# Second feed-forward of a two-layer macaron block: the bias moved from GpSimd into TensorE products, and ScalarE's normalisation of the next group moved ahead

## What is computed

```
x = x + 0.5 * _L0_ffn_ref(_layernorm(x, axis=-1), L0_ffn_kernel, L0_ffn_bias, L0_ffn_a, L0_ffn_b)
...
    w = simulate_quantize_int4(kernel)
    y = jnp.einsum('bsd,df->bsf', x, w) + bias
    lora = jnp.einsum('bsr,rf->bsf', jnp.einsum('bsd,dr->bsr', x, a), b)
    return y + lora
```

```
ri = jnp.concatenate([xf, _stats(xf)], -1)
h = jax.nn.gelu(ri @ r1_w.T + r1_b, approximate=False)
probs = jax.nn.softmax(h @ r2_w.T, -1)
```

## Time and profile before

| | before |
|---|---|
| median of three runs | 1788.64 us |
| profiled execution: its own time | 1788.87 us |
| profiled execution: its span | 1787.2 us |
| TensorE matmul busy in the span | 1488.8 us (83%) |
| VectorE, ScalarE, GpSimd busy | 977.1, 728.9, 564.3 us |
| granted clock of TensorE, mean of the span | 0.908 of full |

### The profile page before, as it was taken

The page is one execution under the profiler, slowest core; times in us unless marked ns, Lnnn a source line. Parts: engine busy times, 40 slices in busy tenths (PEclk is TensorE's granted clock), DMA queues, the critical chain, the costliest instruction groups (busy, mean ns, idle before and its releaser), DMA issues. The chain is left out here.

```text
span 1787.2 us, 27066 instructions
## 1 busy us (share of the span) xinstructions
PE 1488.8 (83%) x9512; PEld 1127.3 (63%) x9512; DVE 977.1 (55%) x2816; ACT 728.9 (41%) x1775; POOL 564.3 (32%) x467
## 2 busy tenths in 40 slices
PE   6899989999999678339999997489995459999994
PEld 5566544555554454229889997255553349899994
DVE  8865677787873597855531111356566855521110
ACT  5222147666667375415423232114333425322331
POOL 6522210000000442321636455221211231636535
PEclk9989889999999898559999999699997569999997
DMA  3034363333300022325969894401112326879974
GB/s 104 18 127 129 107 131 63 79 55 79 55 26 1 12 95 83 150 44 174 246 194 258 245 246 65 133 25 35 48 36 95 118 71 201 225 221 247 265 193 47
DMA packets 113493, 212.11 MB, mean 119 GB/s; under 512 B 20085, under 2 KB 79386, under 8 KB 104154
## 3 DMA queue, kind: packets, MB, share of 16 engines
q1 hardware_dynamic: 87066, 178.93, 31.8%
q0 software_dynamic: 26304, 31.60, 11.4%
HBM read 158.71 MB, written 51.38 MB: 118 GB/s over the span
## 5 line engine op out<-in xcount | busy, mean ns | idle before, releaser
L952 DVE TENSOR_REDUCE attnm_top<-psum 128x1 f32<-128x384 f32 (+3 forms) x384 | 212.8, 597 | 56.4 <-PE psum L1037 52.3
L1174 ACT ACTIVATE attnm_prob<-psum 128x512 f32<-128x512 f32 (+1 forms) x384 | 192.1, 530 | 87.6 <-PE psum L1047 81.0
L2328 POOL DMA_INDIRECT x_sum<-moe1e_y,moe_scatter_i x76 | 119.7, 1575 | 128.2 <-ACT moe1e_y L2462 71.0
L2507 DVE SCALAR_TENSOR_TENSOR moe1e_h<-moe1e_gate,psum 128x160 f32<-128x160 f32 x160 | 50.6, 321 | 199.4 <-ACT moe1e_gate L2436 199.1
L2328 POOL DMA_INDIRECT out<-moe2e_y,moe_scatter_i x76 | 119.2, 1568 | 127.7 <-ACT moe2e_y L2462 70.5
L2507 DVE SCALAR_TENSOR_TENSOR moe2e_h<-moe2e_gate,psum 128x160 f32<-128x160 f32 x160 | 50.4, 321 | 198.8 <-ACT moe2e_gate L2436 198.6
L2383 PE MATMUL psum<-moe1e_xgT,moe_w_up 128*128 128x160 f32 x1024 | 152.2, 304 | 2.4 <-ACT moe1e_xgT L2452 2.4
L2383 PE MATMUL psum<-moe2e_xgT,moe_w_up 128*128 128x160 f32 x1024 | 150.7, 302 | 2.4 <-ACT moe2e_xgT L2452 2.4
L2383 PEld LDWEIGHTS psum<-moe1e_xgT,moe_w_up 128*128 128x128 f32 x1024 | 144.2, 193 | 4.8 <-issue 4.8
L2383 PEld LDWEIGHTS psum<-moe2e_xgT,moe_w_up 128*128 128x128 f32 x1024 | 142.7, 192 | 4.8 <-issue 4.8
L1348 POOL DMA_INDIRECT moe_xg<-xn_rows,moe_gather_i x80 | 84.3, 1054 | 159.3 <-DVE moe_gather_i L1536 93.0
(11 more groups left out here) (414 smaller groups left out, 3230.5 us busy)
## 6 DMA issues: line engine op xcount, KB each, us to landing
moe_w_up<-in_expert_up SPq DMA_DIRECT2D x64, 1024.0 KB, 7.5
moe_w_down<-in_expert_down SPq DMA_DIRECT2D x64, 512.0 KB, 3.5
attnm_q_hat<-q_parts SPq DMA_DIRECT2D x72, 128.0 KB, 4.4
moe_a_up<-in_adapter_up SPq DMA_DIRECT2D x32, 256.0 KB, 4.2
q_parts<-attnf_q_part SPq DMA_DIRECT2D x12, 512.0 KB, 2.8
attnm_k_hat<-k_parts SPq DMA_DIRECT2D x72, 64.0 KB, 2.3
x_res<-in_x SPq DMA_DIRECT2D x8, 512.0 KB, 9.4
v_tails<-attnf_v_tail SPq DMA_DIRECT2D x4, 1024.0 KB, 4.3
```

Of the source, the lines that this page charges most:

```text
L952: nc.vector.tensor_reduce(top[:, n // QUADS % 2, tiles[0]:tiles[-1] + 1, hh:hh + 1], s.ps[:, u.bank, 0:len(tiles) * width].rearrange("p (t ...
L1174: nc.scalar.activation(prob[:, i % NPROB, at:GROUP], s.ps[:, u.bank, at:GROUP], ACT.Exp).then_inc(taken[u.bank], 1)
L2328: nc.gpsimd.indirect_dma_start(total, bass.IndirectOffsetOnAxis(ap=rows, axis=0), y[:, q, k, :], None, bounds_check=TOKENS + SPARE - 1, oo ...
L2507: nc.vector.scalar_tensor_tensor(out=h[:, n % 2, i, :], in0=gate[:, i, :], scalar=1.0 if i < INTER // P else SCALE_A, in1=s.ps[:, u.bank, ...
```

## The change

The bias is no longer added by GpSimd. GpSimd clears a tile `ffn_bias_row` of 128 partitions and copies the bias into its partition 0, once. TensorE opens each of the two banks of multiply(g) with a product of 128x512: the stationary side is column 0 of the identity, repeated 128 times (ones in row 0, zeros in the other 127), the moving side is `bias_row`, repeated twice; the eight products with `ffn_w` then add to it. TensorE waits for the row before the first step of its list. update(g) no longer waits for GpSimd. Apart from that, norm(i+3) on ScalarE moves from behind copy_x(i-1) to directly behind copy(i+2).

```diff
+    bias_row = st.sb("bias_row", [P, C])
...
         @block.gpsimd
         def _(pool):
-            def bias(g):
-                pool.wait_ge(normed, g + 1)
-                xg = s.x[:, GT * g:GT * g + GT, :]
-                nc.gpsimd.tensor_tensor(xg, xg, s.ffn_bias[:].rearrange("p (o c) -> p o c", o=1)
-                                        .broadcast_to([P, GT, C]), ALU.add).then_inc(biased, 1)
-
             for n, part in enumerate(PARTLY):
...
-            bias(0)
-            bias(1)
+            nc.gpsimd.memset(bias_row[:], 0.0).then_inc(cleared, 1)
+            pool.wait_ge(cleared, 1)
+            nc.gpsimd.tensor_copy(bias_row[0:1, :], s.ffn_bias[0:1, :]).then_inc(row_made, 1)
             for i in range(GROUPS):
-                if i + 2 < GROUPS:
-                    bias(i + 2)
                 r.rstd(pool, i)
...
-                v.wait_ge(biased, g + 1)
...
-                for k in range(GT):
-                    for c in range(CC):
-                        mm = nc.tensor.matmul(s.ps[:, u.bank + k // 2, (k % 2) * C:(k % 2 + 1) * C],
-                                              xnT[:, g % 2, c, k * P:(k + 1) * P], s.ffn_w[:, c, :],
-                                              start=(c == 0), stop=(c == CC - 1))
+                for a in range(2):
+                    nc.tensor.matmul(s.ps[:, u.bank + a, :].rearrange("p (h c) -> p h c", c=C), s.ident[:, 0:1].broadcast_to([P, P]),
+                                     bias_row[:].rearrange("p (o c) -> p o c", o=1).broadcast_to([P, 2, C]),
+                                     start=True, stop=False, skip_group_check=True)
+                    for k in range(2 * a, 2 * a + 2):
+                        for c in range(CC):
+                            mm = nc.tensor.matmul(s.ps[:, u.bank + a, (k % 2) * C:(k % 2 + 1) * C],
+                                                  xnT[:, g % 2, c, k * P:(k + 1) * P], s.ffn_w[:, c, :],
+                                                  start=False, stop=(c == CC - 1), skip_group_check=True)
...
+            pe.wait_ge(row_made, 1)
             for what, g in ORDER:
...
                 if 0 <= i + 2 < GROUPS:
                     copy(i + 2)
+                if 0 <= i + 3 < GROUPS:
+                    norm(i + 3)
                 if 0 <= i - 1 < GROUPS:
                     r.absolute(act, i - 1)
...
                     r.copy_x(act, i - 1)
-                if 0 <= i + 3 < GROUPS:
-                    norm(i + 3)
```

More of the change, by code:

```diff
@@ L1892, in ffn_router @@
     shift = st.sb("shift", [P, TILES])
+    bias_row = st.sb("bias_row", [P, C])
     r = RouterFront(nc, st, s, m)
     sem = st.sem
-    all_var, all_rstd, shifted, normed, biased, dve = (sem(n) for n in ("all_var", "all_rstd", "shifted", "normed", "biased", "dve"))
+    all_var, all_rstd, shifted, normed, cleared, row_made, dve = (
+        sem(n) for n in ("all_var", "all_rstd", "shifted", "normed", "cleared", "row_made", "dve"))
     banks = Banks(st)
```

## The result

The changed kernel takes 1796.14 us (median of nine runs, 1793.78 to 1803.79) against 1787.43 of the kernel before (nine runs); the ratio is 1.0043, 95% interval 1.003 to 1.0055. In a second series the changed kernel had 1.0061 (1.0041 to 1.0081). It is slower, by 8 us in the first series and 11 in the second; forecast were 10 (1799, 0.6%), counted from the 1788.64 us of the first three runs of the kernel before. The profiled execution took 1799.05 us.

A forecast was written before the change was run, and what follows sets the result against it. Rounds were taken to close over TensorE and ScalarE, not VectorE. update(7) was 4.26 + 3.26 + 0.73 + 1.73 = +9.98 us; 1788.87 + 10.0 gave about 1799, own range 1796 to 1801, 8-in-10 range 1794.5 to 1803.

The forecast's parts named there:

- The row: Start of the stage: TensorE waits for the bias row ahead of turn(0), +2.6 us (2.4 to 2.8).
- The products: In multiply: 0.865 us a product, 1.73 us a group; update(0) at +4.6 us, update(1) at +6.3.
- the dear product: Rival in multiply: a repeated column or row makes a product cost 1.7 us instead of 0.865; 1807 us, chance 0.03.
- What comes back at the first router turn: Before hidden(0): rnorm(1) takes 1.38 instead of 3.42 us, −2.04, so hidden(0) is at +4.26; not all 5.84 us returns.
- Norm in the loop: Rounds hidden(0) to hidden(2): norm between copy and absolute on ScalarE makes them 12.25 and 12.63 us, together +3.26.
- The round of hidden(3) and the last multiply: TensorE's list sets the round, 11.29 against 10.56 us, +0.73; multiply(7) costs 1.73 in full; update(7) at +9.98.
- the list of signs: What the changed profile would show, including hidden(0) at 648.4, then rounds of 12.3, 12.6, 11.3 and 10.4 us.
- The tail, "as before": Behind update(7): finish(5), hidden(5) to hidden(7), take(7), one chain of the three engines, unchanged by the change.
- VectorE was the bound: Rival: rounds close over VectorE, rnorm(1) to rnorm(4) each give 2.05 us, 5.84 returns; −7.7, about 1781 us, chance 0.05.
- No change: Rival: norm is free since absolute still waits for rnorm, early turn(4) gives back more; +2.7, about 1791.5 us, chance 0.08.
- Slower still, the clock: Rival: TensorE's clock falls once at waits before turn_s(0), hidden(0) or hidden(1); +2 to +4, 1801 to 1803 us, chance 0.17.

The follow-up runs named there:

- The late wait: Changed kernel with TensorE's wait for the bias row moved from ahead of turn(0) to its first reader in multiply(0); ratio 1.0055.
- the kernel without the bias: Kernel before with GpSimd's additions of the bias taken out, nothing in their place, norm at its old place; ratio 1.0001 (0.999 to 1.0012).
- the version built from the results: Kernel before with absolute(7) ahead of gelu(5), norm(4) alone ahead, copy_s ahead of count, GpSimd's bias additions behind its two powers; ratio 0.9963.

## Why the prediction was right

Point by point, counted from the start of the stage:

- **The row.** +2.5 us at turn(0), expected +2.6. The copy of one partition took 0.39 us. The late wait takes it back, 2.0 us of it at hidden(5).
- **The products.** L1989 starts 0.86 us ahead of the L1994 behind it (663.45 to 664.31), expected 0.865. A column of the identity repeated 128 times and a row repeated twice cost nothing extra; the dear product is out. update(0) +4.8, update(1) +6.5 (expected +4.6, +6.3); in the second trace +5.7 and +7.4, since the clock rose later inside multiply(0) (the first four products with `ffn_w` took 3.19 us instead of 2.34), so this term too is known to 1 us only.
- **What comes back at the first router turn.** turn(4) follows turn_x(0) at once; hidden(0) is at +4.5 (+5.3 in the second trace), expected +4.3. Of the 5.84 us the change keeps only rnorm's 2.04, since VectorE set the pace.
- **Norm in the loop.** The rounds are 11.63 and 12.53 us, expected 12.25 and 12.63. That the two rounds grow by norm's 2 us is shown by the two kernels with the norm move and no products, whose rounds are the same once the half clock is taken out. The first was over-priced by 0.6: I had left the load of ScalarE's table ahead of gelu(0), 1.28 us, in the chain. Before, norm(5) and the load put gelu(0) 4.00 us behind hidden(0). Now the load runs at once behind copy_x, while ScalarE waits for hidden, still leaves a wait of 1.04 us, and gelu(0) starts 3.05 us behind hidden(0):

```profile
647.77 1.28 ACT L1784 ACT_TABLE_LOAD   x1
...
650.10 0.69 ACT L1784 ACTIVATE ffn_r_hT<-psum,r1b 128x512 f32<-128x512 f32 x1 [1.04 <-PE psum L1818]
```

- **The round of hidden(3) and the last multiply.** 11.40 us (expected 11.29) and 10.57 (the list of signs has 10.4; 8.92 before + 1.73 would be 10.65); update(7) +9.6, expected +10.0.
- **The tail, "as before".** This is the term that was wrong. From hidden(5) to hidden(7) it took 14.4 us in the first trace and 19.1 in the second, against 17.1; so the stage as a whole was +7.5 and +12.1 us around an expected +10. What differs is the clock. hidden(6) takes 1.95 us in the first trace and 3.75 in the second, after the same wait. That the forecast of the time came within 3 us of the median is owed in part to taking 17.1 for a constant that lies in between, and so in part to luck. The mechanism up to hidden(5) is not: there every term is within 0.6 us in the first trace and within 1.1 in the second. hidden(6) in the first and in the second trace:

```profile
711.79 1.95 PE L1817 MATMUL psum<-ffn_r_xnT,r 128*128 128x512 f32 x4 [3.58 <-ACT ffn_r_statT L1777]
```

```profile
716.31 3.75 PE L1817 MATMUL psum<-ffn_r_xnT,r 128*128 128x512 f32 x4 [3.58 <-ACT ffn_r_statT L1777]
```

- **The rivals.** "VectorE was the bound" is refuted by the kernel without the bias. "No change" expected absolute to wait for rnorm, in the rounds it does not: rnorm(2) stands behind update(3), not update(2) as written there, and is still done at 650.41, ahead of absolute(2) at 654.00. "Slower still, the clock" did not happen in the rounds of the changed kernel: I had put TensorE's waits there at 1.8 to 2.2 us and they are 1.46 before turn_s(0) and 0.66 to 1.12 before hidden, with a granted clock of 1.00 from 642 to 690. It did happen in the two kernels that have the norm move without the products, and at hidden(0) of the version built from the results. One reading behind this rival was too short: the trace of the kernel before has a fall after a wait shorter than the 0.96 us that I took for harmless, hidden(7) after 0.86 us (see the last section).

One thing stays open. In time the norm move alone is no cheaper than the whole change (1.0059 against 1.0043 and 1.0061), though its trace is 4.8 us ahead at hidden(5). The clock in the rounds does not explain it, since those falls are already in that trace's +4.8; against the first trace of the change the difference is made up in the tail (18.6 us against 14.4), against the second only in part ("next" at +9.2 against +12.1). The same order without the bias was at +9.9 at hidden(5) in its trace, so executions with the norm move and no products seem to differ there by several us. Shown are the waits, the clock and the lengths of the rounds in single traces; how often the clock falls over many executions, and so what share of the 10.6 us it makes, is not.

The Trainium skill, SBUF — State Buffer, Who interferes with whom, is borne out as to the mechanism: rnorm was 2 us shorter whenever no addition met it, and in the kernel before one of the four instructions of rnorm(3) took 2.46 us instead of 0.41, ending at 660.52 beside an addition that ended at 660.37. What it cost this kernel is no more than the 2 us that the interval of the kernel without the bias leaves open.

## What to carry to other kernels

Before moving a step on an engine, close the loop of the round: follow who waits for whom until the chain comes back to the same instruction one group later. A step outside of it, that runs while its engine would wait anyway, is free where it stands; inside it costs up to its full length (norm about 2 us, or 1.1 where TensorE's list was nearly as long). VectorE's 8 us of contention, with no place in the loop, were worth nothing that the times can tell. At the stage's end look for work that is ready (rnorm(7) at 694) behind an instruction that waits (gelu(5) until 699): that reordering alone gave 4 us, where the change of this case cost 8 to 11.

## What the runs showed of the hardware

- After TensorE had waited 2.84 to 2.99 us its clock was sometimes at 1.2 GHz and sometimes at 2.4 GHz: in the norm move alone, two waits of 2.85 and 2.84 us, the first followed by 3.36 us for the products of hidden, the second by 1.96. After 3.58 us it was either, too (hidden(6) of the changed kernel, above).
- The length of the last wait does not decide it. After waits of 0.66 to 1.64 us in the rounds I saw no fall, but hidden(7), after 0.86 us, ran at half clock in both kernels, in the changed one right behind 4.4 us of work at full clock (granted clock 1.00 from 711.8 to 716.2, 0.53 from 717.1 to 720.5), which themselves had followed a wait of 3.58 us. hidden(7) in the changed kernel and what stands ahead of it:

```profile
715.64 0.60 PE L1808 MATMUL psum<-ident,ffn_r_stat 128*5 128x128 f32 x4
717.10 3.53 PE L1817 MATMUL psum<-ffn_r_xnT,r 128*128 128x512 f32 x4 [0.86 <-ACT ffn_r_statT L1777]
```

and in the kernel before:

```profile
711.75 3.43 PE L1817 MATMUL psum<-ffn_r_xnT,r 128*128 128x512 f32 x4 [0.86 <-ACT ffn_r_statT L1777]
```

- GpSimd's additions slowed neither VectorE's two reductions L1733 and L1734 (1.22 and 1.21 us beside an addition in the version built from the results, as alone) nor an update that reads PSUM (update(0) of the kernel before, 1.22 us with an addition from 617.60 to 619.96); they slowed a copy of 128x8 from 0.16 to 0.92 us.
- The table load of ScalarE does not wait for the operand of its gelu: in the changed kernel it ran at 647.77, 2.3 us ahead of the gelu and before the products of hidden(0) had ended.
